# SyncE issues the second batch's minus-maximum rows ahead of two weight-block loads

## The reference

```python
def _mha(q, k, v):                      # k = v = the context, q = layernorm(x)
    scores = jnp.einsum('bhqd,bhkd->bhqk', qh, kh) / math.sqrt(hd)
    scores = jnp.where(causal[None, None], scores, jnp.asarray(MASKED_BIAS, scores.dtype))
    attn = jax.nn.softmax(scores, axis=-1)
    out = jnp.einsum('bhqk,bhkd->bhqd', attn, vh)
...
for e in range(E):
    Ye = _gelu(x @ w1[e] + b1[e]) @ w2[e] + b2[e]
```

## Time and profile before

| what | value |
|---|---|
| median of 3 runs | 414.98 us (414.34 to 416.11) |
| profiled execution, its own time | 412.41 us |
| span of that execution in the trace | 410.6 us |
| mean granted TensorE clock over the span | 0.91 of full |
| busy: PE / DVE / ACT / POOL | 321.0 / 306.0 / 268.2 / 180.4 us |
| chain that ended last: PE / DVE / DMA / issue / ACT | 42 / 28 / 10 / 9 / 8 % |

### The profile page before, as it was taken

One profiled execution on the slowest core, in us unless ns is written; L12 is line 12 of the kernel. 1 busy time (PEld: TensorE's weight loads), 2 busy tenths in 40 slices (PEclk: granted clock), 3 DMA queues, 4 the chain that ended last, 5 costly groups with the idle time before them and its releaser, 6 DMA issues.

```text
span 410.6 us, 8728 instructions
## 1 busy us (share of the span) xinstructions
PE 321.0 (78%) x2708; PEld 222.1 (54%) x2709; DVE 306.0 (75%) x745; ACT 268.2 (65%) x540; POOL 180.4 (44%) x245
## 2 busy tenths in 40 slices
PE   0075989989799986878777224698999999999991
PEld 0053337664377654556444113475777777777760
DVE  4998997783954663897998885586777777888760
ACT  1825766725676486989798665652677777777770
POOL 3051305391384067433747459410444554444432
PEclk9997999989989998999977756697999999999997
DMA  5950002851095069130416449455677777778522
GB/s 176 388 222 0 2 0 107 126 147 59 4 225 158 15 85 221 46 117 2 119 42 206 126 102 329 154 219 177 184 254 248 255 200 255 210 253 254 154 26 26
DMA packets 27298, 60.48 MB, mean 147 GB/s; under 512 B 4305, under 2 KB 17954, under 8 KB 24066
## 3 DMA queue, kind: packets, MB, share of 16 engines
q1 hardware_dynamic: 20658, 53.20, 40.2%
q0 software_dynamic: 4416, 6.13, 9.3%
q10 hardware_dynamic: 2192, 0.75, 0.7%
HBM read 29.00 MB, written 6.85 MB: 87 GB/s over the span
## 4 chain that ended last, share of the span: by engine, by line
PE 42%; DVE 28%; DMA 10%; issue 9%; ACT 8%; POOL 2%; ACTq 1%; SPq 0%; DVEq 0%; POOLq 0%
PE bank L1270 8%; PE bank L1637 6%; PE bank L1655 6%; DMA out_dram<-arena,SI 5%; DVE MX L2000 3%; PE bank L1640 3%; PE bank L1658 3%; DMA STG<-in_l_w_dram 2%; PE bank L1356 2%; PE bank L1231 2%; DMA arena<-NMS 2%; PE bank L1382 2%; DVE stats L1720 2%; PE bank L1378 1%; ACT arena L1131 1%
## 5 line engine op out<-in xcount | busy, mean ns | idle before, releaser
L1655 PE MATMUL bank<-arena 128*128 x184 | 63.4, 390 | 2.6 <-DVE X L2274 1.1
L1131 ACT ACTIVATE arena<-arena,B1D 128x128 f32<-128x128 f32 x184 | 57.4, 391 | 8.6 <-DVE arena L2287 8.1
L2287 DVE TENSOR_REDUCE arena<-bank 128x256 f32<-128x512 f32 x92 | 57.3, 680 | 3.1 <-PE bank L1640 3.1
L685 POOL TENSOR_TENSOR W<-STG,W 128x256 f16<-128x256 f32 x64 | 42.7, 700 | 33.4 <-ACT W L882 28.9
L782 POOL DMA_INDIRECT out_dram<-arena,SI x23 | 36.4, 1584 | 36.2 <-DMA out_dram<-arena,SI 16.9
L1658 PE MATMUL bank<-arena 128*128 x184 | 51.3, 279 | 0.0
L685 POOL TENSOR_TENSOR arena<-STG,arena 128x256 f16<-128x256 f32 x56 | 37.3, 700 | 30.2 <-ACT arena L882 28.8
L1637 PE MATMUL bank<-arena 128*128 128x256 f16 x256 | 46.4, 282 | 1.6 <-DVE arena L2250 1.6
L769 POOL DMA_INDIRECT arena<-token_rows,GI x23 | 22.8, 993 | 53.3 <-ACT WS L1125 45.1
L2292 DVE SCALAR_TENSOR_TENSOR arena<-arena 128x512 f16<-128x512 f32 x46 | 29.7, 688 | 21.8 <-ACT arena L1138 21.8
L1640 PE MATMUL bank<-arena 128*128 128x128 f16 x256 | 45.3, 225 | 0.0
(11 more groups left out here) (280 smaller groups left out, 722.3 us busy)
## 6 DMA issues: line engine op xcount, KB each, us to landing
STG<-in_l_w_dram SPq DMA_DIRECT2D x32, 512.0 KB, 4.0
arena<-W SPq DMA_DIRECT2D x16, 1024.0 KB
STG<-W SPq DMA_DIRECT2D x7, 1024.0 KB
arena<-in_l_w_dram SPq DMA_DIRECT2D x2, 1280.0 KB, 7.5
k_parts<-W SPq DMA_DIRECT2D x2, 768.0 KB, 4.4
arena<-k_parts SPq DMA_DIRECT2D x12, 128.0 KB, 5.2
X<-in_x_dram SPq DMA_DIRECT2D x2, 512.0 KB, 7.4
W<-in_ctx_dram SPq DMA_DIRECT2D x1, 1024.0 KB, 10.2
```

The costliest lines, as they stand in the source:

```text
L685: ins = nc.gpsimd.tensor_tensor(l, src, h, ALU.subtract)
L1131: ins = nc.scalar.activation(x, x, ACT.Gelu, bias=B1D[:, e, c:c + 1], scale=1.0 / (X_SCALE * W_SCALE))
L1655: nc.tensor.matmul(bank[6 + q][:, :], GDL[:, q, 0, c * P:(c + 1) * P], W2[:, e, c].rearrange("p s d -> p (s d)"), start=(c == 0), stop=Fal ...
L2287: v.tensor_reduce(half, o, AX.X, ALU.add).then_inc(s_dadd, 1)
```

## The change

One call moves up past one loop in SyncE's list. The wait inside it (`s_nms`, for ACT's copy L981) moves along, and so do its three DMAs.

```diff
             load_weights(13)
             sp.wait_ge(s_down, T)
             load_k_stack(2)
+            load_minus_max(1)
             for i in range(14, 16):
                 load_weights(i)
-            load_minus_max(1)
             load_k_stack(3)
             for i in range(16, 18):
                 load_weights(i)
```

## The result

The changed kernel takes 408.62 us (median of 9 runs, 405.77 to 412.02); the kernel before takes 412.98 us over the 9 runs beside them (410.94 to 416.11). The ratio is 0.9899, 95% interval 0.9867 to 0.9931: faster by 1.0%. Two later rounds of runs of the same file gave 0.9896 both times (0.9828 to 0.9965, and 0.9869 to 0.9923). The forecast was 412.6 with a range from 411.0. It had the direction right and the size, 2.4 us, about half of what it is, and the time lies outside the range. Half of the 4.0 us between forecast and time is the base: over 9 runs the kernel before is 2.0 us faster than in the 3 runs that the forecast was added to. But with the right base too the range would have begun at 409.1 (412.98 - 3.9), above the time.

A forecast was written before the change was run, and what follows sets the result against it. It took the kernel to be bound by a stall of all three fast engines on late NMS rows. A 2.4 us gain at the transposes, all other costs 0, off the 414.98 us median gave 412.6 us, range 411.0 to 415.2.

The forecast's parts named there:

- What bounds the kernel: Near 158 us TensorE, VectorE and ACT stand still for the NMS rows; TensorE idles 3.96 us, on the path.
- why the rows land late: Rows of 8 KB take 6.3 us to land, behind key stack and weight blocks 14 and 15 in SyncE's issue order.
- Step 1: SyncE meets the wait for ACT's copy at 150.06; rows still issue at 151.89, at no cost on TensorE.
- Step 2: Batch 1's rows land between 155.3 and 156.6, taken as 156.0; landing 2.2 to 3.5 us after issue.
- Step 3: Batch 2's transposes then wait for ACT's L963, for any landing up to 157.1; gain 2.33 to 2.53, taken as 2.4 us.
- Steps 4 and 5: Weight blocks 14 and 15 issue 3.6 us later, the last key stack 0.9 us later; cost 0 each.
- Step 6: Everything behind the stall moves forward by the same 2.4 us.
- Rival A: TensorE's clock stays up after the shorter idle time: gain 3.3 us, 411.7 us; chance 0.18.
- Rivals B: Rows land late anyway, held by the key stack or the transfers now following: gain 0 to 1, 414.5 us; chance 0.14.
- C: TensorE meets more low clock later, in the stretch from 260 to 300: slower, 415.9 us; chance 0.09.
- D: The stall is not on the path and is made up elsewhere: same time, 414.98 us; chance 0.07.

The follow-up runs named there:

- TensorE filled: Kernel before, with 16 matmuls of 512 columns, results never read, put ahead of TensorE's wait for batch 1's rows: ratio 0.9979.
- nothing behind: Kernel before, with the last batch's key stack moved behind weight block 16, so nothing is issued right after the rows: ratio 0.9981.
- ACT's parts first: ACT's repetition of query parts put ahead of its store of the values product: on the changed kernel 0.9851, again 0.9869; on the kernel before 1.0015.
- rows amid the key stack: Changed kernel, with the rows issued ahead of the last two of the six key DMAs: ratio 0.9899.

## Why the prediction was wrong in size

**Where the time goes.** Over the four traces with both blocks in front (the one with TensorE filled left out) the stretch has a mean of 18.0 us, over the three of the change 14.3: 3.7 us. Of these 2.9 us are the start of the transposes (13.03 against 10.13) and 0.8 us the way from there to the first `maximum` (4.97 against 4.17). The ratio of 0.9896, of 412.7 us, stands for 4.3 us, interval 3.2 to 5.4, so the stretch can hold all of it; the 0.6 us between are not located. The two traces of the kernel before by itself have a mean of 17.7, which would make it 3.4 us: read the stretch as 3.4 to 3.7. The first pair's further 3.9 us (6.7 - 2.8) are not of the change's making as far as the traces tell: 1.31 us arose ahead of it, and later stretches differ as much between two traces of one kernel (73.68 and 76.03 us from batch 3's first `maximum` to the first L2287 in two traces of the changed one).

**What bounds the kernel, and why the rows land late: right.** TensorE, ScalarE and VectorE stood still for the rows, and what SyncE had issued in front of them did it: with nothing behind them they were as late, with one block in front about half the loss is left, with none the transposes start 10.07 to 10.91 us behind the last `maximum`, with both 12.38 to 13.81. But "behind them in the queue" was too narrow: on another queue they were as late.

**Step 1, the wait moved at no cost: right.** The rows leave 4.18 us behind the last `maximum` in both kernels.

**Step 2, the landing: its range ended too early.** It bounded the landing by 2.2 to 3.5 us after issue; the three traces have 3.4, 4.3 and 4.9. What it left out is the q8 packet, seen here too, in 0.3 us of the time in which the rows' packets move (first, second, third trace):

```profile
q8 instruction: 1, 0.02, 22.8%
...
q8 instruction: 1, 0.02, 38.4%
...
q8 instruction: 1, 0.02, 40.1%
```

These are 1.09, 1.84 and 1.92 us, in the order of the landings. In the first trace no packet of the key stack was left from 152.75 on, and the third row still landed at 155.2, so there the key stack was not what held it. In these three traces it cost little: the transposes start at most 0.16 us later (10.23 against 10.07). The two traces with ACT's parts first, where the third row took 4.9 us each time, have 10.65 and 10.91.

**Step 3: the order is right, its size is the term that failed.** L963 released the transposes in the first trace of the change, and in the other two the rows came hardly later than it: 10.07, 10.09 and 10.23 us. The other end of the difference, "160.09 - 157.76 = 2.33", was wrong: 160.09 is the start of the transposes behind one stall of 3.96 us in one execution. The other traces with both blocks in front and nothing to fill the wait have landings of 7.1 to 7.4 and idle times of 4.75 to 5.02 us. The length of a wait for a crowded transfer was taken from one execution as if it were the duration of an instruction. With the mean of the four traces the same step would have given 2.9. That the first pair gained 12.38 - 10.07 = 2.31 us is the forecast's own trace used again, not a second proof of the size. A detail was off as well: L1407 and L1410 take 0.34 us at full clock (159.15 to 159.49), not 0.62, which moves the bound from 157.1 to 157.4.

**Steps 4 and 5, the blocks and the key stack come later at no cost: right.** In the three traces no scaling by ACT in batch 1 waited for a block, and the stretch from batch 2's first `maximum` to batch 3's is 21.3 to 21.9 us before and after.

**Step 6 and the sum: the clock was put at nothing.** Step 6 let the rest move forward by the same 2.4 us, with no term for TensorE's clock; the traces have 0.8 us there (next paragraph). The two terms, 2.9 and 0.8, are the 3.7 us of the stretch. That nothing is lost behind it is not contradicted, but the later stretches vary too much to show it.

**Rival A (the clock stays up) was in these traces not a rival but a second term, with 0.18 given to it.** In all five traces with both blocks in front the first 16 transposes took 1.91 us, at 1.2 GHz; in the three of the change they took 1.06 to 1.09. The cost up to the first `maximum` was 4.64 to 5.22 us, now 4.05 to 4.25. I had counted 0.9 us for it and found 0.8, but had put it in another case than the forecast. It needs no clock that stays up for the whole stage: in the second trace of the change the clock fell at 158.9, behind the first transposes, and the way was 4.25 us. How regular the term is, is open: of the seven traces with no block in front two had the transposes at 1.91 us too (ACT's parts first, again, and rows amid the key stack), and the one with one block had them at 1.06. The rule of the Trainium skill that I had quoted beside it ("TensorE: Matmul & The Clock Gate", section "What's actually happening": activity releases the throttle) points the same way as the means, but single traces do not follow the length of the wait: 1.06 us behind 3.74 us of idle time, 1.91 behind 2.50.

**Rivals B, C and D** did not come. B's doubt had a grain of truth, since the rows still take 3.4 to 4.9 us behind the key stack where 1.8 is the least; part of that is the q8 packet.

## What to carry to other kernels

A small DMA that an engine waits for should be issued before bulk loads that nobody waits for yet, even if a wait for a semaphore comes to stand in front of the bulk loads: check only that these still land before their first use. It can be overdone: ahead of the key stack too, the rows came early and the keys late, and nothing was left of the gain (0.9990). A second queue was no substitute in the one run that tried it. When a stall behind other transfers is priced from a trace, its length is one draw: take a second trace of the same program, or let the range reach well above it, and put what the idle time may do to TensorE's clock into the sum.

## What was not expected of the hardware

- DMAs of 8 KB within SBUF landed in 1.8 us with nothing in front (one in 3.3), the longest of three after 3.4 to 5.0 us behind 768 KB of keys, 6.1 us behind these and one block of 512 KB, 6.5 to 8.2 us behind these and two.
- On ACT's queue, with SyncE's blocks and keys under way, they took 7.7 to 7.8 us, and their packets all moved within 156 to 157 us, 4.5 us and more behind their issue.
- One packet of the queue that the profile calls "instruction" took 0.9 to 2.0 us of one DMA engine. Where it came among the rows' packets, the last piece of a row started when it had ended (154.12 against 154.13 in the first trace of the change, 158.07 against 158.09 with nothing behind).
- 3.63 us of extra matmuls in a wait of TensorE did not keep the clock at 2.4 GHz; it fell to 1.2 GHz at 160.8, behind 2.06 us of idle time.
